# A fused two-layer shifted-window transformer: the order of VectorE's work around the GELU of a group of tiles

## What is computed

```
xn   = layernorm(x)
qkv  = xn @ w_qkv + b_qkv
attn = softmax(q k^T * scale + relative bias + shift mask)   (bias and mask in block 0 only)
x    = x + (attn @ v) @ w_proj + b_proj
h    = gelu(layernorm(x) @ w_fc1 + b_fc1)                    (768 hidden channels)
x    = x + h @ w_fc2 + b_fc2
```

## Time and profile before

| what | value |
|---|---|
| runs | 4489.7, 4492.06, 4493.99 us; median 4492.06 |
| profiled execution | 4490.49 us, span 4488.7 us |
| mean granted TensorE clock | 0.904 |
| TensorE matmul busy | 88% of the span |
| VectorE busy | 77% |
| GpSimd busy | 75% |
| ScalarE busy | 61% |
| DMA engines, transposes and loads | 76.0% |

### The profile page before, as it was taken

The page is one execution under the profiler, slowest core; times in us unless marked ns, Lnnn a source line. Parts: engine busy times, 40 slices in busy tenths (PEclk is TensorE's granted clock), DMA queues, the critical chain, the costliest instruction groups (busy, mean ns, idle before and its releaser), DMA issues. The chain is left out here.

```text
span 4488.7 us, 170135 instructions
## 1 busy us (share of the span) xinstructions
PE 3937.7 (88%) x62800; PEld 2783.4 (62%) x62800; DVE 3454.4 (77%) x9093; ACT 2729.8 (61%) x5921; POOL 3358.2 (75%) x6257
## 2 busy tenths in 40 slices
PE   3888988988999899899889889998998898898888
PEld 2556666666666666666666666666666666666665
DVE  5777777777777777777777777777777777777776
ACT  1566666666666666666666666666666666666665
POOL 4777777777777777777777777777777777777775
PEclk9899998999899899989989998998999899899899
DMA  4877887887788688778867877887787788678775
GB/s 101 148 136 143 143 140 140 141 143 140 138 144 141 137 142 144 136 141 142 142 139 140 142 140 140 141 145 137 143 141 137 142 140 144 141 142 138 135 134 101
DMA packets 2347958, 622.14 MB, mean 139 GB/s; under 512 B 2244598, under 2 KB 2345338, under 8 KB 2347132
## 3 DMA queue, kind: packets, MB, share of 16 engines
q1 hardware_dynamic: 2347132, 611.27, 76.0%
HBM read 32.15 MB, written 25.17 MB: 13 GB/s over the span
## 5 line engine op out<-in xcount | busy, mean ns | idle before, releaser
L1040 POOL TENSOR_TENSOR rstd<-vare,half 128x2 f32<-128x2 f32 x520 | 589.6, 1134 | 663.7 <-DVE vare L877 663.6
L579 PE MATMUL ps_h<-xh,w_fc 128*128 128x512 f16 x3840 | 892.4, 379 | 42.0 <-ACT scaled L700 42.0
L595 PE MATMUL ps_h<-w_fc,hid 128*128 128x192 f16 x9216 | 839.4, 249 | 0.0
L595 PEld LDWEIGHTS ps_h<-w_fc,hid 128*128 128x128 f16 x9216 | 792.4, 100 | 58.1 <-issue 36.5
L685 ACT ACTIVATE stage<-ps_s 128x768 f32<-128x768 f32 x512 | 414.9, 810 | 606.7 <-PE ps_s L537 606.3
L936 DVE TENSOR_TENSOR hid<-scaled,hid 128x512 f16<-128x512 f32 x768 | 668.3, 895 | 143.0 <-POOL hid L1103 136.0
L1103 POOL TENSOR_SCALAR hid<-scaled 128x512 f16<-128x512 f32 x768 | 523.4, 692 | 275.8 <-ACT scaled L700 275.3
L663 ACT ACTIVATE xs<-xn 128x192 f16<-128x192 f32 x512 | 184.6, 361 | 863.6 <-POOL xn L1047 863.6
L579 PEld LDWEIGHTS ps_h<-xh,w_fc 128*128 128x128 f16 x3840 | 361.7, 97 | 485.9 <-ACT scaled L700 154.0
L474 PE MATMUL bank<-w_qkv,xh 128*128 128x384 f16 x2560 | 607.0, 377 | 25.7 <-DMA xh<-xs 13.6
L474 PE MATMUL bank<-w_proj,ot 128*128 128x192 f16 x2560 | 349.6, 276 | 261.2 <-DVE o_tok L916 257.2
(11 more groups left out here) (112 smaller groups left out, 6912.7 us busy)
## 6 DMA issues: line engine op xcount, KB each, us to landing
x_img<-in_x_dram SPq DMA_DIRECT2D x256, 96.0 KB, 2.2
out_dram<-y_img SPq DMA_DIRECT2D x256, 96.0 KB, 2.0
xh<-xs SPq DMA_TRANSPOSE x520, 2.6
qkt<-qk SPq DMA_TRANSPOSE x512, 4.4
pt<-stage SPq DMA_TRANSPOSE x512, 4.1
ot<-os SPq DMA_TRANSPOSE x512, 2.3
stage<-in_L_conv_fc_w_dram SPq DMA_DIRECT2D x2, 384.0 KB, 4.3
stage<-in_L_conv_w_fc_dram SPq DMA_DIRECT2D x2, 384.0 KB, 3.7
```

Of the source, the lines that this page charges most:

```text
L579: last = mm(ps_h[:, u % 2, :].rearrange("p (a t) -> p a t", a=GROUP), w_fc1[layer][:, part, m * 128:(m + 1) * 128], xh[:, p % 2 * GROUP:(p ...
L595: mm(bank[:, 0:C], hid16[:, hs, m, tok], w_fc2[layer][:, ws, m, :], start=(m == 0 and i == 0), stop=False)
L1040: g_.tensor_tensor(rstd[:, m % 2, :], vare[:, m % 2, :], half[:, :].broadcast_to([128, 2]), ALU.pow)\
```

## The change

Only VectorE's order inside a step is rewritten; no instruction, wait, buffer or other engine's order changes.

- Place 0: `v_lo` and the statistics of the visit six steps ahead come right behind `row_max`, in front of the attention residual; before, `v_lo` stood behind it and these statistics at the step's end.
- Place 1: before, low halves 2 and 3 open the step, 4 stands between `inverse_sums` and `o_norm`, 5 behind `v_lo`. Now `mean_variance`, `inverse_sums`, `o_norm` and `row_max` come first, half 2 behind `row_max`, half 3 behind the second `mean_variance`, half 4 behind `centre`, half 5 behind `qk_lo`.
- Places 2 and 3 keep their order.

```diff
                 mlp = 0 <= p < PHASES
-                if mlp and place == 1:
-                    hidden_lo(2)
-                    hidden_lo(3)
+                early = mlp and place == 0
                 if live(s + 5):
                     mean_variance(s + 5, 0)
                 if live(s - 2):
                     inverse_sums(s - 2)
-                if mlp and place == 1:
-                    hidden_lo(4)
-                if live(s - 2):
                     o_norm(s - 2)
                 if live(s):
                     row_max(s)
+                if early and live(s):
+                    v_lo(s)
+                if early and live(s + 6):
+                    statistics(s + 6, 0)
+                if mlp and place == 1:
+                    hidden_lo(2)
                 if live(s - 3):
                     attention_residual(s - 3)
                     statistics(s - 3, 1)
-                if live(s):
+                if live(s) and not early:
                     v_lo(s)
-                if mlp and place == 1:
-                    hidden_lo(5)
                 if live(s - 3):
                     mean_variance(s - 3, 1)
+                if mlp and place == 1:
+                    hidden_lo(3)
                 if live(s + 5) or live(s - 3):
                     centre(s + 5)
-                if mlp and place == 0:
+                if mlp and place == 1:
+                    hidden_lo(4)
+                if early:
                     hidden_lo(0)
                     hidden_lo(1)
                 if live(s):
                     p_lo(s)
                 if live(s + 3):
                     qk_lo(s + 3)
+                if mlp and place == 1:
+                    hidden_lo(5)
                 if mlp and place >= 2:
                     mlp_residual(p * GROUP + 2 * place - 4)
                     mlp_residual(p * GROUP + 2 * place - 3)
-                if live(s + 6):
+                if live(s + 6) and not early:
                     statistics(s + 6, 0)
```

## The result

The changed kernel takes 4445.79 us (median of 4 runs, 4445.51 to 4446.41) against 4492.16 for the kernel before on the same chips: ratio 0.9897, interval 0.988 to 0.9914, 46 us faster. The forecast was faster, 4418, range 4365 to 4497.

A forecast was written before the change was run, and what follows sets the result against it. TensorE, 88% busy, was taken to set the time except where it waits, chiefly for VectorE's o_norm; 1.8 gained less 1.2 for the low clock, 0.58 us over 127 groups, took 74 us off: 4418, range 4365 to 4497.

The forecast's parts named there:

- The wait moves: TensorE's 2.03 us wait per group before step B's projection goes; about 2.5 us before step C's q/k product replaces it.
- Step C: Third of a group's four steps, with the second MLP product; its first mlp_out was to start 1.2 us earlier.
- VectorE's gain up to step C's row maximum: VectorE reaches that row maximum only 0.3 us earlier, since the moved low halves still stand ahead of it.
- the port rule: Two-input VectorE and SBUF-reading GpSimd instructions exclude each other, so spreading halves over a busy GpSimd wins nothing; not in the sum.
- Full-clock gain of TensorE: Earlier mlp_out, 1.2 and 2.1 us in alternate groups, mean 1.65, plus 0.13 for its low-clock piece: 1.8 a group.
- low clock: TensorE at 1.2 instead of 2.4 GHz after its idle hole; cost taken as 1.2 us a group, between 0 and 2.4.
- step B: Second of a group's four steps, where VectorE's rewritten order lets row_max start at 2004.55 instead of 2007.50.
- Net: Gain of 1.8 less 1.2 us for the clock, 0.58 a group over 127 groups: 74 us.
- The rival of the beat: Clock falls keep a 34.13 us beat and take the whole gain back: same time, 4485 to 4497; chance 0.31.
- The hidden fall: The low-clock stretch runs out inside TensorE's idle hole, so all 1.8 us a group is kept: 4263; chance 0.06.
- The slower case: The low-clock stretch reaches past 2018.0 into mlp_out; at 2019.2 it costs 2.4, +0.6 us a group, 4568; chance 0.07.
- Step A: First of a group's four steps, making GELU pieces 0 to 3; VectorE's new order there was to change 0.

The follow-up runs named there:

- changed kernel with its hole filled: Eight matmuls of unused result added to the changed kernel in TensorE's idle time before step C's q/k product; 4276.73 us, ratio 0.9523.
- the best order: Changed kernel with low half 5 and late statistics behind step C's row maximum, plus eight idle-time matmuls before its q/k product; 4266.6 us.

## Why the prediction was right

*The wait moves.* By its words the projection's wait goes and 2 to 3 us of waiting for `qk_lo` come; measured 2.21 in the group shown and 232.2 us in 124 waits. Step C's q/k product was to come 1.2 earlier; in the group shown it came 1.5 earlier. Against the group's GELU table load the first `mlp_out` starts 1.40 earlier in this group (17.92 behind it, 19.32 before) and 0.75 earlier in the next (19.81, 20.56 before), where 0.8 to 1.2 was said. The mean group, 33.79, is below 34.0 as said.

*VectorE's gain up to step C's row maximum.* I took 0.3 out of -0.1 to 0.9; it is 0.73. Halves 3 and 4 took 0.74 and 0.68, where the sum had 0.85 for the one that was added to the 0.69; half 5 took 0.87. Beside halves 3 and 4 GpSimd was near the end of `o_lo`, idle, or had started `scale` after VectorE. GpSimd's lines, to be held against the halves at 1991.20 and 1992.01:

```profile
1990.85 0.55 POOL L1081 TENSOR_TENSOR os<-o_tok,os 128x192 f16<-128x192 f32 x1
1992.24 1.00 POOL L1045 TENSOR_TENSOR rstd<-vare,half 128x2 f32<-128x2 f32 x1 [0.84 <-DVE vare L877]
```

The mean of all 768 halves is 802 ns where it was 895, and the high halves' on GpSimd 618 ns for 692:

```profile
L936 DVE TENSOR_TENSOR hid<-scaled,hid 128x512 f16<-128x512 f32 x768 | 606.2, 802 | 106.7 <-POOL hid L1108 106.6
L1108 POOL TENSOR_SCALAR hid<-scaled 128x512 f16<-128x512 f32 x768 | 466.5, 618 | 276.8 <-ACT scaled L700 276.3
```

So spreading the halves did win time on both engines, where the prediction's reading of the port rule leaned to nothing. The Trainium skill (SBUF — State Buffer, Who interferes with whom) says that such instructions exclude each other. These rows agree with it: a half took 0.98 beside a subtraction of GpSimd that had started before it (1988.69), and 0.68 where `scale` started after it. Exclusion still leaves a gain where the new place puts a half beside an idle GpSimd; that was left out of the sum.

*Full-clock gain of TensorE.* Predicted 1.8 a group, 229 us. Before to changed kernel with its hole filled is 4492 - 4277 = 215 us, 1.7 a group; by the pair of groups without a fall it is 1.82 (34.13 less 32.31). That it fits this well is in part luck, for VectorE gained 0.4 more than taken and the sum should have come out higher. A wait that the prediction didn't have took that back. In every second group an image transpose stands on TensorE in step C. The output transpose behind it uses the same bank and must wait until ScalarE has copied the image transpose out, and ScalarE's copy stands behind its copy for the second norm, which waits for GpSimd. The changed kernel, ScalarE and VectorE in the group of the GELU table load at 2011.58:

```profile
2028.70 0.36 ACT L663 ACTIVATE xs<-xn 128x192 f16<-128x192 f32 x1 [4.31 <-POOL xn L1052]
2028.97 0.31 ACT L658 ACTIVATE x_new<-bank 128x192 f32<-128x192 f32 x1
```

```profile
2028.14 0.95 DVE L899 TENSOR_REDUCE smax<-ps_s 128x12 bf16<-128x768 f32 x1
2030.99 0.36 DVE L923 SCALAR_TENSOR_TENSOR x_tok<-bank,x_tok 128x192 f32<-128x192 f32 x1 [1.90 <-PE bank L476]
```

`o_norm` is done at 2028.23, the row maximum at 2029.09, but the projection starts at 2029.79 and the residual 1.90 late: the transposes' chain, not VectorE, is last there. The kernel before had the same chain, in the group of the earlier trace rows:

```profile
2048.20 0.31 ACT L658 ACTIVATE x_new<-bank 128x192 f32<-128x192 f32 x1
2048.57 0.66 PE L604 MATMUL bank<-ident,x_tok 128*96 128x128 f32 x2
```

The output transpose starts 0.06 behind the copy's end (2048.51). The prediction put the residual's wait of 1.95 in this group down to the low clock alone and let the full clock bring `mlp_out` to 2048.4, before the transpose that stands ahead of it. Measured from step B's q/k product in the changed kernel with its hole filled, `mlp_out` comes 1.97 earlier in such a group than before (10.29 behind it for 12.26) and 1.56 in one of the other kind (9.61 for 11.17); the prediction had 2.1 and 1.2. With 0.4 more from VectorE both would have been higher, and only that of the other kind is. This wait is read from the traces; no run took it away.

*The low clock.* I took 1.2 a group; by the filled hole it is 1.33 (169 us / 127), by the groups without a fall 1.4 to 1.5. It is the largest single term against the gain, and the choice between 0 and 2.4 was the weakest step: a value between a short and a long fall, which no row supported more than its neighbours. The kernel before had paid 0.9 to 1.0 already, so the low clock took about 0.5 a group, some 60 us, out of the 100 us that the order is worth at full clock. About 40 are left; measured are 46.

*Net.* 0.58 a group predicted, 0.36 measured: 46 us over 127 groups for the 74 forecast. By the times of the runs the gross was 0.1 too high and the low clock 0.13 too low; both point the same way. By the groups without a fall the gross was right and the low clock carries all of the error, 0.2 to 0.3. Either way the term that was mis-sized is the low clock.

*The rival of the beat.* Its premise is right: the beat is the clock's, though single groups don't keep it, as the rival says they do. Its consequence came in part: in some stretches the changed kernel stands on the beat (the pair of 68.29), in others not (67.71), and the mean is 33.79. It was close: 0.43 us more work in a group puts the changed kernel back on 34.134 us. Of the 0.43 it paid 0.34.

*The hidden fall* (4263) did not happen by itself, yet the filled hole comes to 4277. *The slower case*: in the group of the GELU table load at 2011.58 the low stretch reaches 2034.85, 3.5 us behind the start of `mlp_out`, about as far as the rival asked for; in the group before it, it ends at that start.

*Step A*: 0 predicted, 4492.15 against 4493.98 measured.

## What to carry to other kernels

When a reordering moves a wait, look at where TensorE's idle time goes as well as at its length: with a hole of some 2.2 us in either kernel, the low clock cost at least 80 us in the one and at least 169 in the other, where the hole comes later. When the mean length of many groups stays the same to the third digit while their work differs, test with a small known load; if it costs nothing, small gains may bring nothing either, until they are large enough to leave the beat. When a filler brings the clock up, count the falls that are left before the difference of two such runs is called the difference at full clock. And price a moved instruction at its new neighbours: beside a GpSimd that was idle or started later a half took 0.68, beside a busy one 0.98.

## What the runs showed that I had not expected

- Three kernels whose dense work differs by up to 0.43 us a group run at a mean of 34.13 us a group over 100 groups, two of them at 34.134 to the third digit, while single groups of the kernel before take 33.60 and 34.66.
- Matmuls that compute nothing, in TensorE's idle time alone, make the changed kernel 169 us (3.8%) faster at a mean granted clock of 0.996 instead of 0.926, and the best order with them stands at 4266.6 us, 5.0% under the kernel before.
